# A decoder layer on one core: the experts' first norm taken in the cross attention, the experts' steps in another order

## The reference, cut to what matters

```python
x = layernorm(x + self_attention(x))            # B, N, C = 8, 512, 256; 16 heads, relative bias
x = layernorm(x + cross_attention(x, ctx, ctx)) # this result is called x2 in the kernel
# experts, on the 4096 tokens of x2:
assign = argmax(x2 @ centroids.T)               # 8 experts
alpha = sigmoid(best affinity)
h = relu(layernorm(x2, ln_g[e], ln_b[e]) @ w1[e].T + b1[e])      # 256 -> 1024
ye = x2 + h @ w2[e].T + b2[e]                                    # 1024 -> 256
out = layernorm(x2 + (alpha * ye + (1 - alpha) * x2))
```

## Time and profile before

| | |
|---|---|
| median of 3 runs | 1068.13 us (1065.26 to 1069.1) |
| the profiled execution, its own time | 1071.02 us |
| its span, first to last instruction | 1069.2 us |
| PE / ACT / DVE / POOL busy | 88% / 72% / 63% / 33% |
| mean granted TensorE clock | 0.937 |

### The profile page before, as it was taken

One profiled execution on the slowest core, in us unless ns is written; L12 is line 12 of the kernel. 1 busy time (PEld: TensorE's weight loads), 2 busy tenths in 40 slices (PEclk: granted clock), 3 DMA queues, 4 the chain that ended last, 5 costly groups with the idle time before them and its releaser, 6 DMA issues. The chain is left out here.

```text
span 1069.2 us, 17528 instructions
## 1 busy us (share of the span) xinstructions
PE 942.3 (88%) x5301; PEld 523.5 (49%) x5301; DVE 675.9 (63%) x1760; ACT 772.8 (72%) x1452; POOL 347.9 (33%) x340
## 2 busy tenths in 40 slices
PE   5599999999999999999999999962599889898891
PEld 2233444444444433333333333321599779888790
DVE  5276877777777777354546464753377667667672
ACT  1387777787877868899989898940478767686670
POOL 4043133140313111001112211221436666665664
PEclk9699999999999989999999999985699999898895
DMA  8988587978769576695587558400523334333441
GB/s 210 201 229 235 120 249 143 320 153 243 201 154 275 103 195 109 148 266 110 123 151 153 105 117 160 100 20 28 197 91 119 105 110 176 105 117 115 127 169 44
DMA packets 73546, 162.93 MB, mean 152 GB/s; under 512 B 16441, under 2 KB 40056, under 8 KB 63416
## 3 DMA queue, kind: packets, MB, share of 16 engines
q1 hardware_dynamic: 68088, 152.23, 56.5%
q0 software_dynamic: 5056, 9.20, 3.0%
q10 hardware_dynamic: 320, 0.52, 0.1%
HBM read 116.40 MB, written 49.54 MB: 155 GB/s over the span
## 5 line engine op out<-in xcount | busy, mean ns | idle before, releaser
L717 ACT ACTIVATE probs<-sc 128x512 f32<-128x512 f32 x1024 | 528.5, 607 | 110.6 <-DVE sc L799 82.7
L491 PE MATMUL sc<-qst,kst 57*128 57x512 f32 (+1 forms) x1024 | 269.5, 471 | 18.0 <-DMA qst<-s_qk 12.4
L799 DVE TENSOR_TENSOR sc<-sc,strip 128x308 f32<-128x308 f32 (+1 forms) x512 | 192.9, 429 | 101.7 <-PE sc L491 100.8
L503 PE MATMUL ot<-probs,vals 128*32 128x512 f32 x1600 | 215.0, 610 | 0.0
L491 PEld LDWEIGHTS sc<-qst,kst 57*128 57x128 f32 (+1 forms) x1024 | 118.1, 186 | 193.0 <-ACT probs L717 147.9
L1753 POOL DMA_INDIRECT f_rows<-s_x,f_get_ids x45 | 107.0, 2378 | 36.4 <-issue 34.8
L1611 ACT ACTIVATE f_h<-f_h_ps,f_par 128x384 f32<-128x384 f32 x104 | 64.0, 616 | 27.0 <-PE f_h_ps L1530 26.9
L1691 DVE TENSOR_TENSOR f_h_lo<-f_h,f_h_hi 128x384 fp32r<-128x384 f32 x104 | 56.9, 547 | 27.8 <-ACT f_h_hi L1612 27.4
L1189 POOL TENSOR_SCALAR veps<-mv_self 128x4 f32<-128x4 f32 x8 | 1.9, 232 | 192.3 <-DVE mv_self L857 192.3
L1612 ACT ACTIVATE f_h_hi<-f_h_ps,f_par 128x384 fp32r<-128x384 f32 x104 | 64.3, 618 | 0.0
L1252 POOL DMA_INDIRECT s_tokens<-ids,place_i x32 | 32.9, 1029 | 88.9 <-DVE place_i L943 81.6
(11 more groups left out here) (173 smaller groups left out, 1672.8 us busy)
## 6 DMA issues: line engine op xcount, KB each, us to landing
s_qk<-w_hi SPq DMA_DIRECT2D x32, 512.0 KB, 7.1
strip<-in_w_all SPq DMA_DIRECT2D x16, 1024.0 KB, 11.8
f_raw<-in_w_all SPq DMA_DIRECT2D x14, 1024.0 KB
kst<-s_qk SPq DMA_DIRECT2D x32, 256.0 KB, 6.1
qst<-s_qk SPq DMA_DIRECT2D x32, 256.0 KB, 7.4
s_x_parts<-split SPq DMA_DIRECT2D x16, 512.0 KB, 8.6
kst<-s_ctx_parts SPq DMA_DIRECT2D x32, 256.0 KB, 6.1
qst<-s_x_parts SPq DMA_DIRECT2D x32, 256.0 KB, 7.3
```

The lines of the kernel that those rows point to most:

```text
L491: nc.tensor.matmul(sc[j][:], kst[at:at + rows, i, P * c:P * c + P], qst[at:at + rows, i, :], start=True, stop=True).then_inc(scored, 1)
L503: last = nc.tensor.matmul(sums_bank(n, g)[32 * j:32 * j + 32, :], vals[:, c, 4 * g + j, :], probs[:, k % KEPT, j, :], start=(c == 0), stop ...
L717: nc.scalar.activation(probs[:, k % KEPT, j, :], sc[j][:], ACT.Exp, scale=scale).then_inc(exped, 1)
L799: nc.vector.tensor_tensor(sc[j][:, lo:hi], sc[j][:, lo:hi], band_backwards(rank_of(4 * g + j), at, hi - lo), ALU.add).then_inc(biased, 1)
```

## The change

- x2's row gets 256 more values: the row less its mean over its deviation (ROW = 2C + 1 = 513). `stats_of_x2` (blocks 9 and 10), POOL's `inverse_deviation_h`, and `hat_x2` (block 14) make it in the cross attention, so x2's store and every gathered row are twice as long. The store of x2 of batch c-2 is issued in the first blocks of batch c.
- The experts' `norm_in`, `hat_in` and their POOL part are gone; `turn_in` reads the gathered row.
- ACT's second relu (L1612) is gone; DVE makes the rounded part by a copy in `split_h`. `hat_out` goes from DVE to ACT (at f = 7), `keep_rows` from DVE to POOL. The weights are split in four pieces of 1024 columns, spread over f = 0, 1, 3, 4 (ACT) and 1, 2, 5, 7 (DVE).
- POOL's step begins with the gather, SP's put list comes last.
- The end of the last batch and of the last tile go chunk by chunk. The first two get lists, the parameters of expert 0, identity and constants are loaded or made before the barrier, the semaphores of the second part are never cleared in between, and the last batch's `list_tokens` stands behind the test for the exact branch.

```diff
-ROW = C + 1
+ROW = 2 * C + 1
 # sync, cross_body(c)
                 if c < B - 1:
                     load_context(c + 1)
+                if c > 1:
+                    store_x2(c - 2)
                 load_x1(c)
+                if c < B - 1:
+                    load_pair(n + 1, 0)
                 if c == 0:
-                    load_pair(n + 1, 0)
                     store_x1(B - 1)
-                if c > 0:
-                    if c < B - 1:
-                        load_pair(n + 1, 0)
-                    store_x2(c - 1)
                 if c < B - 1:
                     load_pair(n + 1, 1)
+                else:
+                    store_x2(c - 1)
...
 # vector, cross
+            def hat_x2(c):
+                dve.wait_ge(h_rstd, c + 1)
+                for t in range(NC):
+                    last = nc.vector.tensor_scalar(x2[:, t, C + 1:ROW], x2[:, t, 0:C], mv_h[:, t, 0:1], rstd_h[:, t:t + 1], ALU.subtract, ALU.mult)
+                last.then_inc(have_hat, 1)
...
+            add_x2(B - 1, 0)
             for t in range(NC):
-                add_x2(B - 1, t)
+                if t + 1 < NC:
+                    add_x2(B - 1, t + 1)
+                norm_x2_last(t)
+            stats_of_x2(B - 1, range(NC))
...
-            norm_x2(B - 1)
-            for i in range(2):
-                keep_x2T(B - 1, i)
+            choose(B - 1)
             judge()
-            choose(B - 1)
             give_places(B - 1)
...
 # sync, behind the attention
+            store_last(sp)
+            sp.dma_start(par[0][:], io["params"][0]).then_inc(early["ld_par0"], 16)
+            sp.wait_ge(st_last_ids, 16 * NC)
+            sp.wait_ge(pstep, 15)
+            for i in range(2):
+                first_list = sp.value_load(plan[0:1, 1, i:i + 1], min_val=0, max_val=E * FULL_LIST - 1)
+                sp.dma_start(get_ids[i][:], scratch["tokens"].rearrange("(l p n) o -> l p (n o)", p=P, n=TC * STEP)[bass.ds(first_list, 1)]
+                             .rearrange("l p n -> (l p) n")).then_inc(early["ld_get"][i], 16)
+            sp.wait_ge(st_x2, 16 * B)
...
 # experts: sync
                 load_params(i + 1, 1 - s)
-                if not isinstance(i, int) or i > 0:
-                    load_put(i - 1)
                 load_ids(i + 2, s, n + 1)
                 load_w(i + 2, s)
+                if later(i):
+                    load_put(i - 1)
...
 # experts: vector
+            def split_h(i, f):
+                at = f % (LAG + 1)
+                dve.wait_ge(h_full, FC * i + f + 1)
+                wait(dve, y_mm, FC * i + f - LAG)
+                nc.vector.tensor_copy(h_hi[at][:], h[at][:]).then_inc(h_hi_ready, 1)
+                wait(dve, h_hi_ready, FC * i + f + 1, dve_passed)
+                nc.vector.tensor_tensor(h_lo[at][:], h[at][:], h_hi[at][:].bitcast(F32), ALU.subtract).then_inc(h_ready, 1)
...
+            def step(i, s, n):
+                for f in range(FC):
+                    split_h(i, f)
+                    if f in (1, 2):
+                        low_w(i + 1, 1 - s, 0, f - 1, w1_lo_ready)
+                    if later(i) and f == 3:
+                        add_rows(i - 1, 1 - s)
+                    if later(i) and f == 4:
+                        norm_out(i - 1)
+                    if f in (5, 7):
+                        low_w(i + 1, 1 - s, 1, f // 7, w2_lo_ready)
+                    if f == 6:
+                        if later(i):
+                            shift_rows(i - 1)
+                        low_in(i + 1, 1 - s)
...
 # experts: gpsimd
+            def keep_rows(i, s, n):
+
+                wait(pool, gathered[s], 16 * TC * (n + 1), pool_passed)
+                wait(pool, have_res, i - 1, pool_passed)
+                wait(pool, have_gated, 2 * (i - 1), pool_passed)
+                nc.gpsimd.tensor_copy(keep[s][:], rows[s][:, :, 0:C + 1]).then_inc(kept, 1)
...
             def step(i, s, n):
-                rstd_of(i + 1, mv_in, mv_in_ready, veps_in, rstd_in, have_xhat, have_rstd_in)
-                if not isinstance(i, int) or i > 0:
-                    rstd_of(i - 1, mv_out, mv_out_ready, veps_out, rstd_out, have_out, have_rstd_out)
                 gather(i + 2, s, n + 1)
-                if not isinstance(i, int) or i > 0:
-                    scatter(i - 1)
+                keep_rows(i + 1, 1 - s, n + s)
+                if later(i):
+                    inverse_deviation(i - 1)
+                    scatter_rows(i - 1)
...
 # experts: scalar
             def relu(i, s, f):
                 act.wait_ge(h_mm, FC * i + f + 1)
-                wait(act, y_mm, FC * i + f - LAG)
+                wait(act, h_ready, FC * i + f - LAG)
                 bias = par[s][:, 2 * DC + f:2 * DC + f + 1]
                 nc.scalar.activation(h[f % (LAG + 1)][:], h_ps[f % (LAG + 1)][:], ACT.Relu, bias=bias).then_inc(h_full, 1)
-                nc.scalar.activation(h_hi[f % (LAG + 1)][:], h_ps[f % (LAG + 1)][:], ACT.Relu, bias=bias).then_inc(h_hi_ready, 1)
```

More of the change, by code:

```diff
@@ L1243, in split_x @@
                 nc.gpsimd.tensor_tensor(x_lo[:], xT[:], x_hi[:].bitcast(F32), ALU.subtract).then_inc(x_lo_ready, 1)
[L1245 to L1253, removed]
-                        in_=ids[:, t:t + 1], in_offset=None).then_inc(st_ids, 16)
             def peek(n):
@@ L1378, in expert_ffn @@
         w_hi, w_lo = halves
-        par = two("par", [P, PARAMS])
-        rows = two("rows", [P, TC, ROW])
-        get_ids = two("get_ids", [P, TC * STEP], I32)
-        keep = two("keep", [P, TC, ROW])
+        par, rows, get_ids = early["par"], early["rows"], early["get_ids"]
+        keep = two("keep", [P, TC, C + 1])
         xn_hi = two("xn_hi", [P, DC, TILE], F32R)
@@ L1455, in tiles, with later @@
             return count
+        def later(i):
+            return not isinstance(i, int) or i > 0
         list_of = scratch["tokens"].rearrange("(l p n) o -> l p (n o)", p=P, n=TC * STEP)
@@ L1573, in step, with split_w @@
                         ffn2(i, s, f - LAG)
-                    if f == 1 and (not isinstance(i, int) or i > 0):
+                    if f == 1 and later(i):
                         turn_out(i - 1)
                     if f == 4:
-                        turn_in(i + 1)
+                        turn_in(i + 1, 1 - s, n + s)
                 for f in range(FC - LAG, FC):
                     ffn2(i, s, f)
-            pe.wait_ge(ld_ident, 16)
-            turn_in(0)
-            tiles(pe, step, lambda i, s: turn_out(i - 1))
+            turn_in(0, 0, 0)
+            tiles(pe, step, lambda i, s: turn_last(i - 1))
         @block.scalar
         def _(act):
-            def split_w(i, s, n, m):
-                act.wait_ge(ld_w[s], 32 * (n + s))
-                wait(act, y_mm, FC * (i - 1))
-                nc.scalar.activation(w_hi[s][:, m, :], raw[s][:, m, :], ACT.Copy).then_inc(w_hi_ready, 1)
+            def split_w(i, s, n, m, part):
+                some = slice(F * part, F * part + F)
+                if part == 0:
+                    act.wait_ge(ld_w[s], 32 * (n + s))
+                    wait(act, y_mm, FC * (i - 1))
+                nc.scalar.activation(w_hi[s][:, m, some], raw[s][:, m, some], ACT.Copy).then_inc(w_hi_ready, 1)
             def scale_in(i, s, n):
@@ L1714, in step @@
-            def step(i, s, n):
-                later = not isinstance(i, int) or i > 0
-                for f in range(FC):
-                    low_h(i, f)
-                    if f == 0:
-                        norm_in(i + 1, 1 - s, n + s)
-                    if f == 1:
-                        hat_in(i + 1, 1 - s)
-                    if later and f == 2:
-                        norm_out(i - 1, 1 - s)
-                    if f == 3:
-                        keep_rows(i + 1, 1 - s)
-                    if later and f == 4:
-                        hat_out(i - 1)
-                    if f == 5:
-                        low_in(i + 1, 1 - s)
-                    if f == 6:
-                        low_w1(i + 1, 1 - s)
-                    if f == 7:
-                        low_w2(i + 1, 1 - s)
```

392 lines of the change are left out of this document (243 added, 149 removed).

## The result

The changed kernel takes 1053.37 us (median of 4 runs, 1049.96 to 1055.11), the kernel before 1068.25 beside it: a ratio of 0.987, 95% interval 0.984 to 0.991. So it is faster by 14.9 us, 1.3%, where 50 us were forecast, and it is 13 us above the range. That is little, but clear of the noise. The profiled execution has a span of 1053.2 us, 16.0 less than before.

| stretch | before | after | difference | forecast |
|---|---|---|---|---|
| start to the first batch's places | 495.3 | 498.4 | +3.1 | 0 |
| from there to the last `turned` of the last batch | 215.5 | 227.9 | +12.5 | 0 |
| from there to the experts' first matmul | 51.8 | 44.2 | -7.6 | -7.5 |
| first matmul to the first y | 20.5 | 23.6 | +3.0 | 0 |
| twelve periods | 260.7 | 238.4 | -22.3 | -38.7 |

A forecast was written before the change was run, and what follows sets the result against it. The loop was taken as bound by DVE's order in fast tiles, by late gathers and the clock in slow ones. Terms -38.7 (loop), -7.5 (between stages), -5.5 (end) sum to -51.7, giving 1016.4; forecast 1018 us, range 1005 to 1040.

The forecast's parts named there:

- the loop, -38.7 forecast: Experts' loop: twelve periods of 18.5 us, 222 us against 260.7, with bounds of 18.1 and 20.0 a period.
- the layout of DVE's list: Experts' step timed from PE's first matmul: DVE's f = 1 to 4 done at 11.6, last h at 16.5, needed at 17.05.
- its even tiles' loss: Old loop, tile 8: PE idles 1.36 us before its last ffn2, for an h that DVE made behind `low_w1`.
- cross attention, 0 forecast: Cross attention: DVE gets 3.3 us more per batch of some 36, where it has 18 free; change taken as 0.
- a failing cover of `hat_x2`: Cross attention: if its 1.4 us were not hidden in one block a batch, 8 x 1.4 = 11 us, put into the range.
- PE's floor: Experts' loop: PE's own matmuls and transposes need 18.1 us a period.
- the odd tiles' chain: Old loop, tile 7: late gather delays `norm_in`, `hat_in`, `turn_in`, then the clock drops; 24.2 us against tile 8's 20.0.
- the stretch between the stages: Cross attention to experts: first gather 3.4 us earlier, norm work of 4.5 gone, longer rows give back 0.4; -7.5 us.
- the end: After the last tile: put list loaded 5.0 us after the last y, not 10.6; -5.5 us, or -3.
- POOL is the new wait: Rival, experts' loop: all gathers run blocked, DVE waits at the shift, period 20.0 to 20.8, 1035 to 1045 us; chance 0.2.
- Slower: Rival, experts' loop: first gather shut out 7.7 us in every tile, clock drops, period 24.8, 1092 us; chance 0.06.
- the loop keeps its period: Rival, experts' loop: odd tiles' loss comes from the loop's turn, not the gather; 1044 us; chance 0.05.

The follow-up runs named there:

- e4: The changed kernel with `keep_rows` back on DVE, ahead of `norm_out` at f = 4: 1052.56 us.
- e3: The changed kernel with DVE doing `low_in` and both low pieces of w2 behind the last split of h: 1029.01 us.
- e8: The changed kernel with two tiles of x2 that take turns, so `norm_x2` waits only for the store of two batches before: 1037.75 us.
- e6: The changed kernel with tile 1's weights waiting for the first tile's gather alone: 1049.60 us.
- e9: The changed kernel with x2 doubled, DVE's low pieces behind the last split of h, and tile 1's weights early: 1012.87 us.
- e10: The changed kernel with x2 doubled and DVE's low pieces behind the last split of h; tile 1's weights wait for both gathers: 1011.84 us.

## Why the prediction was right or wrong

**Wrong: the loop, -38.7 forecast and -22.3 measured.** The step that failed is the layout of DVE's list, from "is done at 11.6" to "h of f = 7 at 16.5, against 17.05". The forecast counted 18.1 for this order and then put all its doubt on POOL. (The 18.5 that it took does not follow from its own layout either: with gathers of 2.3, 1.6 and 1.3 POOL's 1/deviation comes at 14.2 and not at 15, and even 0.4 of lateness fits into the 0.55 left at the last ffn2. By its own terms the period was 18.1, and the miss in the loop 21 us instead of 16.) Set against the trace (PE's first matmul of this tile is at 892.06), h of f = 5, 6 and 7 was ready at 14.7, 16.8 and 18.8, not at 12.4, 14.4 and 16.5. Each is 2.3 or 2.4 late:
- The list of f = 1 to 4, from the first weight piece to the variance, takes 9.1 us (896.59 to 905.68), where I had given it 6.3. My own durations already made about 7.2 (two pieces 2.3, the sum of rows 0.95, statistics 1.4, three h of 0.86): I had drawn it too tight by some 0.9. The list also began earlier than I had it, at 4.5 and not at 5.3, or the h would have been later still.
- A rounding and its subtraction take 0.98, not 0.86: the subtraction waits for the rounding, 0.15. The prediction had these pauses in DVE's total ("some 15 with the pauses") and left them out of the order.
- One subtraction takes 1.72 instead of 0.56, at the time of POOL's copy for `keep`. I had costed that copy for POOL alone. No run takes it away alone (e4 trades it for 0.95 of copying on DVE); in e3 it is still 1.72, and the period is at the floor all the same.

DVE's busy time came out at 15.96 us where the sum had 13.9.

A margin of 0.55 us before the last ffn2 can't bear errors of this size. Both the weight piece ahead of h of f = 6 and `low_in` ahead of f = 7 are in my layout, with their 1.15 and 1.1 us. What I passed over is that they were the next tile's work and need not stand there. In the kernel before I had named the same pattern as its even tiles' loss. e3 shows it: behind the last h they cost nothing, and the period is the floor that I had worked out, 18.08 for 18.1.

**Wrong: cross attention, 0 forecast and +12.5 measured up to the last `turned`.** The step is "x2's store of 1 MB instead of 0.5 has from block 2 to block 8 of the next batch". The window was named, but no landing time was set against it. The store is queued behind SP's own wait in `load_context`: in five batches it is issued 6.7 to 7.6 us behind the places, and `norm_x2` wants the tile 14.4 behind them (e8, where nothing holds it). In these 7 us a store of 1 MB would have had to land, and it takes 11.5, so `norm_x2` waits 4 us on average in these batches. I had also kept 11 us in the range for a failing cover of `hat_x2`; that was another mechanism, and no run isolates it. With the doubled tile, where `hat_x2` is still done, the full batches take 35.7 us as before: its cover holds. The longest batch was hit three times, by the wait, by tile 0's weights and by the clock.

**Wrong and small: "The first tile itself I leave at its time"**, +3.0. SP waits for both gathers before it loads tile 1's weights; with that wait shortened the first tile took 21.3 us (e6) and 20.8 (e9), against 23.0 to 25.6 with it. The times of these runs do not show the difference.

**Right.** PE's floor; the odd tiles' chain gather, `norm_in`, `hat_in`, `turn_in` is gone with its clock loss; the stretch between the stages, -7.6 for -7.5, though from parts of another size (the first gather 4.1 earlier for 3.4, from there to the transposes 3.5 for 4.1), so that the match of the sum is in part luck; the end, -4.7 for -5.5.

**The rivals.** "POOL is the new wait" gave 1035 to 1045 and is refuted in its mechanism: the shift never waited, and the period is 19.87 by DVE alone. The Trainium skill, page "SBUF — State Buffer", section "Who interferes with whom", which I weighed there, would have the roundings shut POOL's gathers out. In the tile shown the gathers beside roundings and subtractions took 1.25, 1.07 and 1.26 us, and the longest of the loop 2.08, so that blocking by 2.56 or 7.72 did not come here. The section also leaves it to the order of issue who is blocked, and it infers that a subtraction of two SBUF tiles does not hold up the writing of descriptors; the gather of 7.72 us beside such subtractions speaks against that inference, which my prediction did not say. The page's sentence on a VectorE operation with two SBUF inputs beside a GpSimd instruction that reads SBUF does agree with the subtraction of 1.72 beside POOL's copy, only the one that waited was DVE. "Slower" and "the loop keeps its period" didn't come either. None of my cases had a loss in cross attention with a weight of its own, and this is why the time fell out of the range: with DVE's list alone the sum would have been 1018 + 16 = 1034.

## What to carry to other kernels

Where one engine's list of work is laid out against another's deadlines, put what belongs to the next round behind the last item with a deadline now; it cost nothing here and was worth 21.4 us of the loop, while less work in the bad order was worth 15.7. When a row gets longer, follow its store to whoever overwrites the buffer, from the moment at which the queue can issue it and not from the one at which it is ready. With a second buffer the doubled store cost the full batches nothing (35.7 to 35.9 us in e9 and e10). And give a step that a sum clears by half a microsecond a case of its own in the range.

## What the runs showed of the hardware

- A subtraction of 128x384 on DVE with two inputs in SBUF took 1.72 us instead of 0.56 beside a copy of 771 columns on POOL of 0.83 us. Its extra 1.16 is more than the copy's whole length.
- A rounding and the subtraction that reads its result start 0.50 us apart, with 0.15 idle between, though the rounding takes 0.35.
- Gathers on POOL mostly took 1.0 to 1.3 us beside dense work on DVE here, a few of the first tiles 1.7 to 2.1 (e10's tile 0: 2.06 and 1.69), and 2.56 and 7.72 before. What decides between these no run here tells.
- Stores of 0.5 MB landed in 5.8 us (median) and those of 1 MB in 11.5, in the same place of the same queue.
- With the same instructions and the same idle time of PE in the 20 us ahead, the granted clock fell to 1.2 GHz for some 10 us in one profiled execution and stayed at 2.4 GHz in another.
